# A graph-network kernel: the second node half's first layer, its rounding, lower part and aggregation in two halves of columns

## The chip, the cores and the metric

The kernel runs on one core of one Trainium2 chip. The metric is the device time of one execution in microseconds (us). The engines are called by the profile's names: PE is the matmul engine (PEld its weight loads), DVE the vector engine, ACT the scalar engine, POOL GpSimd, SP the engine that only issues transfers here. They run side by side, each through its own list of instructions in order, and wait for one another by semaphores.

## What is computed

Two layers of a graph network on 256 nodes with 512 features, over 4352 edges. The change sits wholly in the first layer. Cut to that layer:

```python
h = jnp.maximum(_layernorm(x, axis=-1), 0.0)
adj = zeros(256, 256); adj[src, dst] = 1; adj[dst, src] = 1
adj = adj + eye
dinv = 1.0 / sqrt(adj.sum(axis=1))
adj = adj * dinv[:, None] * dinv[None, :]
x = x + adj @ (h @ weight) + bias        # first layer (x @ weight is h @ weight here)
h = jnp.maximum(_layernorm(x, axis=-1), 0.0)
x = x + second_layer(h, src, dst, edge_attr_20, edge_weight, edge_attr_4, ...)
```

The second layer projects `h` to node channels, gathers them by edge, multiplies them by filters computed from the edge attributes, sums the products into the nodes (the scatter), and passes the sums through two more small layers.

## The kernel before, in words

The program is one block per engine, written out by hand: the order of instructions on each engine is the order of the code, and semaphores (the dictionary `q`, with `wait_ge` and `then_inc`) tie the engines together. There are no planners and no pools.

The 256 nodes are two halves of 128 partitions (NH = 2), numbered `a` or `b`; the 512 features are four blocks of 128 (KD = 4). PSUM is eight banks of 512 fp32 columns, and `pair0` to `pair3` are two banks each.

Before the change's place, DVE builds one-hot rows of the edges, PE multiplies them into the adjacency counts (`adjacency`, line 605), and PE transposes the normalised nodes into `h1T`. The first layer of node half 0 (`first_layer(0, ...)`, line 632, into `bank[0]`) is spread between the parts of the adjacency. Then, in this order:

- PE transposes the clipped counts (line 666). DVE makes of them the adjacency matrix `A` and the degrees (lines 465 and 469). PE meanwhile multiplies the first layer of node half 1, `first_layer(1, 0, KD)` (called at line 668): four matmuls of 512 columns in fp32 into `bank[1]`. A program matmul in fp32 shows as two MATMUL records, each with a weight load.
- POOL raises the degrees and variances to the power -0.5 (line 354): first `s1`, the scale of each row of `hW`, then `dinv`.
- ACT rounds `s1 * hW` of each half to fp32r, `hW_hi` (line 251), and DVE takes what the rounding left, `hW_lo` (line 479). Ahead of the latter DVE has two instructions of other work, `xb` (line 472) and `hYlo` (line 475).
- PE aggregates (line 674): for both parts and both halves `b` of the summed nodes, two matmuls of 512 columns (`a` = 0 and 1), into `bank[4]` and `bank[5]`. In the order of the code: high part of half 0, high part of half 1, low part of half 0, low part of half 1. Each of these four waits for its own piece. The last two matmuls raise `L0`.
- PE goes on with the product of two small weights (line 680) and the filters of the first two groups of edges (`filters(0)`, `filters(1)`, lines 649 and 652), and then waits for the next layer's input (`transposes`, line 688).
- DVE forms `x1`, the input of the second layer, once for each half (line 485), as `L0` rises. From there the second layer begins: `h2` (ACT line 257, DVE line 488), the sums of squares (lines 261 and 492), `h2T` (lines 263 and 496), the scale `s2` on POOL (lines 371 and 373), the node channels (line 695), their two parts `HL` (lines 277 and 504), and then the gather (line 721), the products and the scatter (line 733) over nine groups of edges.
- After the rounding ACT copies `y` out over the features for the products (`y_blocks(0, free)`, line 225), and POOL, after its powers, builds a quarter of a one-hot matrix (`node_onehots_late(3)`, line 358).

Of the kernel before, what the change touches and what calls it, by code (L numbers as in the profile page):

```python
# [5 lines left out]
def gnn_preln_kernel(nc, x, idx, dst_row, f_t, yr, w0, bias0, w1, w2, b2, w_in, w_o1s, w_o1vt, w_o2s, w_o2v,  # L6
                     out):
    fp32 = mybir.dt.float32
# [3 lines left out]
    ALU = mybir.AluOpType  # L12
    ACT = mybir.ActivationFunctionType

    P = 128
    N, D = x.shape
    NH = N // P
    KD = D // P
# [35 lines left out]
    with ctx:  # L54
        def sb(name, shape, dt=fp32):
            return ctx.enter_context(nc.sbuf_tensor(name, shape, dt))

        def sem(name):
            return ctx.enter_context(nc.semaphore(name))
# [7 lines left out]
        w0_sb = sb("w0_sb", [P, KD, D])  # L67
# [31 lines left out]
        h1T = sb("h1T", [P, NH, KD, P])  # L99
# [3 lines left out]
        A = sb("A", [P, NH, N], fp32r)  # L103
        deg = sb("deg", [P, 2 * NH])
        scales = sb("scales", [P, 2 * NH])
        dinv, s1 = scales[:, 0:NH], scales[:, NH:2 * NH]
        hW_hi = sb("hW_hi", [P, NH, D], fp32r)
        hW_lo = sb("hW_lo", [P, NH, D], fp32r)
# [29 lines left out]
        bank = [pair[i // 2][:, 512 * (i % 2):512 * (i % 2) + 512] for i in range(8)]  # L138
# [12 lines left out]
        q = {n: sem("s_" + n) for n in names.split()}  # L151
# [45 lines left out]
        def _(act):  # L197
# [48 lines left out]
            act.wait_ge(q["half"], 3)  # L246
            nc.scalar.activation(OdT[:, 1, E // 2:], gap, ACT.Relu, bias=one[:, 0:1], scale=-1.0).then_inc(q["OdTa"], 1)
            act.wait_ge(q["scales"], 1)
            for a in range(NH):
                act.wait_ge(q["hW"], a + 1)  # L250
                nc.scalar.activation(hW_hi[:, a, :], bank[a][:, :], ACT.Copy, scale=s1[:, a:a + 1]).then_inc(q["hW_hi"], 1)
            act.wait_ge(q["OdTa"], 1)
            act.wait_ge(q["adj"], 1)
            act.wait_ge(q["y"], 1)
# [3 lines left out]
                                 scale=-float(D)).then_inc(q["neg_h2"], 1)  # L258
# [16 lines left out]
            for a in range(NH):  # L275
                act.wait_ge(q["H"], a + 1)
                nc.scalar.activation(HL[:, a, 0, :], bank[4 + a][:, 0:C], ACT.Copy,
                                     scale=s2[:, a:a + 1]).then_inc(q["Hh"], 1)
# [126 lines left out]
        def _(dve):  # L405
# [68 lines left out]
            dve.wait_ge(q["hhi"], 2)  # L474
            nc.vector.tensor_tensor(hY[0:64, :], za[64:128, :], hY[64:128, :].bitcast(fp32), ALU.subtract).then_inc(q["hYlo"], 1)
            dve.wait_ge(q["scales"], 1)
            for a in range(NH):
                dve.wait_ge(q["hW_hi"], a + 1)
                nc.vector.scalar_tensor_tensor(hW_lo[:, a, :], bank[a][:, :], s1[:, a:a + 1],
                                               hW_hi[:, a, :].bitcast(fp32), ALU.mult, ALU.subtract).then_inc(q["hW_lo"], 1)  # L480
            dve.wait_ge(q["scales"], 2)
            dve.wait_ge(q["xb"], 1)
            for a in range(NH):
# [111 lines left out]
        def _(pe):  # L595
# [26 lines left out]
            for a in range(NH):  # L622
                pe.wait_ge(q["h1"], a + 1)
                for k in range(KD):
                    last = nc.tensor.transpose(bank[(6, 1)[a]][:, k * P:(k + 1) * P], h1[:, a, k * P:(k + 1) * P], id_sb)
# [3 lines left out]
            def first_layer(a, k0, k1):  # L629
                pe.wait_ge(q["h1T"], a + 1)  # L630
                for k in range(k0, k1):
                    last = nc.tensor.matmul(bank[a][:, :], h1T[:, a, k, :], w0_sb[:, k, :], start=(k == 0), stop=(k == KD - 1))  # L632
                if k1 == KD:
                    last.then_inc(q["hW"], 1)
# [29 lines left out]
            for a in range(NH):  # L664
                for b in range(NH):
                    last = nc.tensor.transpose(bT[:, a * N + b * P:a * N + (b + 1) * P], CI[:, b, a * P:(a + 1) * P], eye_sb[:, 0, 0:P])
            last.then_inc(q["CT"], 1)
            first_layer(1, 0, KD)

            for p, (part, ready) in enumerate(((hW_hi, "hW_hi"), (hW_lo, "hW_lo"))):  # L670
                for b in range(NH):
                    pe.wait_ge(q[ready], b + 1)
                    for a in range(NH):
                        last = nc.tensor.matmul(bank[4 + a][:, :], A[:, b, a * P:(a + 1) * P], part[:, b, :],  # L674
                                                start=(b == 0 and p == 0), stop=(b == NH - 1 and p == 1))
                        if b == NH - 1 and p == 1:
                            last.then_inc(q["L0"], 1)
            pe.wait_ge(d_o1v, 16)
            pe.wait_ge(d_o2v, 16)
# [106 lines left out]
            for a in range(NH):  # L786
# [4 lines left out]
                                 stop=True).then_inc(q["fin"], 1)  # L791
# [66 lines left out]
```

## Time and profile before

| | us |
|---|---|
| median of 3 runs | 71.69 (71.65 to 71.82) |
| the profiled execution | 71.83 |
| its span, first to last instruction | 69.8 |

In that execution PE is busy for 61.7 us (88% of the span), DVE for 60.1 (86%), ACT for 48.6 (70%) and POOL for 39.5 (57%). The granted clock of PE is full in the stretch of the change. The table of busy shares doesn't say what a change of a few matmuls is worth; this is read from the chain of work that ended last and from the order of time around the place.

### The profile page before, as it was taken

Reading aid. Unit: us, or ns where it says so; the run is one execution under the profiler, and the core shown is the slowest. Engines: PE = TensorE matmul, PEld = TensorE weight load, DVE = VectorE, ACT = ScalarE, POOL = GpSimd, SP = SyncE. Lnnn points to the kernel's source line nnn. Section 1 sums busy time; section 2 is a strip of 40 time slices with the busy share of each in tenths; the row PEclk is TensorE's granted clock in tenths of the full one; section 3 lists DMA queues with packets and bytes.
Section 4 is the critical chain, followed back from the end, with each engine's and each line's share of the span. In section 5 each row is a group of like instructions: output and inputs, shape, how many; then the busy total and the mean of one; then the engine's idle time right before and its main releaser. Section 6 shows DMA issues by size and latency. Waiting matters only on the chain.

```text
span 69.8 us, 1215 instructions
## 1 busy us (share of the span) xinstructions
PE 61.7 (88%) x407; PEld 48.6 (70%) x407; DVE 60.1 (86%) x124; ACT 48.6 (70%) x74; POOL 39.5 (57%) x46
## 2 busy tenths in 40 slices
PE   3999998999999999897998979999999999998340
PEld 1236754568834268796987969998898989997220
DVE  4599999999979968989999898989898999972760
ACT  0700059978999697967979999988696969732700
POOL 5000030000676989594799979999999988700000
PEclk9999999999999999999999999999999999999995
DMA  0899998984000000000000000000000000000044
GB/s 1 129 396 247 361 499 379 449 317 124 9 0 0 0 0 0 0 0 5 0 0 0 0 0 9 5 0 0 0 0 0 0 0 9 0 0 0 0 148 153
DMA packets 3049, 5.65 MB, mean 81 GB/s; under 512 B 540, under 2 KB 1936, under 8 KB 2916
## 3 DMA queue, kind: packets, MB, share of 16 engines
q1 hardware_dynamic: 2274, 5.14, 21.3%
q10 hardware_dynamic: 770, 0.44, 2.2%
q8 instruction: 3, 0.05, 0.3%
q14 instruction: 2, 0.02, 0.1%
HBM read 5.06 MB, written 0.52 MB: 80 GB/s over the span
## 4 chain that ended last, share of the span: by engine, by line
DVE 45%; PE 20%; issue 14%; ACT 13%; DMA 3%; DVEq 0%; ACTq 0%
ACT OsR L240 8%; DVE WQ L412 7%; DVE Os L412 7%; PE pair L632 5%; ACT w_sb L284 5%; DVE dst_bc L565 4%; PE pair L733 4%; PE pair L742 4%; DVE pair L514 3%; PE pair L674 3%; DMA idx_sb<-idx 3%; PE pair L721 3%; DVE w_sb L485 2%; DVE za L446 2%; DVE hX L449 2%
## 5 line engine op out<-in xcount | busy, mean ns | idle before, releaser
L733 PE MATMUL pair<-OsR,Mh 128*128 128x256 f32 x56 | 13.6, 281 | 0.0
L733 PE MATMUL pair<-OsR,Ml 128*128 128x256 f32 x56 | 13.6, 281 | 0.0
L721 PE MATMUL pair<-HL,OdT 128*128 128x256 f32 x68 | 10.1, 289 | 1.6 <-DVE dst_bc L565 0.7
L395 POOL TENSOR_TENSOR Ml<-dst_bc,Mh 128x512 fp32r<-128x512 f32 x8 | 10.4, 1305 | 1.1 <-ACT Mh L301 1.0
L721 PEld LDWEIGHTS pair<-HL,OdT 128*128 128x128 f32 x68 | 8.6, 188 | 2.8 <-issue 2.8
L733 PEld LDWEIGHTS pair<-OsR,Ml 128*128 128x128 f32 x56 | 10.5, 188 | 0.0
L733 PEld LDWEIGHTS pair<-OsR,Mh 128*128 128x128 f32 x56 | 10.5, 188 | 0.0
L605 PEld LDWEIGHTS pair<-WQ,Os 128*128 128x128 bf16 x68 | 6.8, 104 | 4.0 <-DVE WQ L412 1.8
L605 PE MATMUL pair<-WQ,Os 128*128 128x256 bf16 x68 | 9.4, 297 | 0.2 <-DVE WQ L412 0.2
L399 POOL TENSOR_TENSOR Ml<-dst_bc,Mh 128x512 fp32r<-128x512 f32 x7 | 9.2, 1309 | 0.0
L240 ACT ACTIVATE OsR<-Os 128x1024 fp32r<-128x1024 bf16 (+1 forms) x9 | 9.0, 999 | 0.0
L632 PE MATMUL pair<-w_sb,h1T 128*128 128x512 f32 x16 | 7.7, 601 | 0.3 <-ACT h1T L214 0.3
L305 ACT ACTIVATE Mh<-dst_bc 128x512 fp32r<-128x512 f32 (+1 forms) x9 | 5.5, 609 | 3.1 <-DVE dst_bc L565 3.0
L514 DVE TENSOR_TENSOR pair<-pair,w_sb 128x512 f32<-128x512 f32 (+1 forms) x10 | 6.2, 619 | 1.3 <-ACT w_sb L284 1.2
L358 POOL TENSOR_SCALAR OdT<-dst_bc,iota_c 128x1088 fp32r<-128x1088 int32 x2 | 6.1, 3054 | 1.6 <-DVE OdT L459 1.4
L341 POOL CAST b2p<-b_sb 96x128 bf16<-96x128 f32 x1 | 1.4, 1402 | 8.3 <-issue 8.3
L534 DVE TENSOR_TENSOR pair<-pair,WQ 128x512 f32<-128x512 f32 (+1 forms) x9 | 6.0, 662 | 0.1
L378 POOL TENSOR_TENSOR WQ<-WQ,y 128x256 f32<-128x256 f32 (+1 forms) x9 | 5.8, 652 | 0.1
L207 ACT ACTIVATE za<-pair 128x512 f32<-128x512 f32 (+1 forms) x3 | 1.4, 489 | 6.3 <-PE pair L613 6.3
L284 ACT ACTIVATE w_sb<-pair 128x512 f32<-128x512 f32 (+1 forms) x10 | 5.2, 518 | 0.8 <-PE pair L721 0.7
L412 DVE TENSOR_TENSOR Os<-iota_r,idp 128x512 bf16<-128x512 bf16 (+3 forms) x7 | 5.6, 796 | 0.0
L412 DVE TENSOR_TENSOR WQ<-iota_r,idp 128x512 bf16<-128x512 bf16 (+3 forms) x7 | 5.6, 796 | 0.0
(122 smaller groups left out, 140.2 us busy)
## 6 DMA issues: line engine op xcount, KB each, us to landing
dst_bc<-dst_row SPq DMA_DIRECT2D x1, 2176.0 KB, 12.9
w_sb<-w SPq DMA_DIRECT2D x1, 1024.0 KB, 8.1
x_sb<-x SPq DMA_DIRECT2D x1, 512.0 KB, 4.4
out<-x_sb SPq DMA_DIRECT2D x2, 192.0 KB, 1.9
f_sb<-f_t SPq DMA_DIRECT2D x1, 378.0 KB
b_sb<-bias SPq DMA_DIRECT2D x1, 256.0 KB, 13.1
w_sb<-w ACTq DMA_DIRECT2D x1, 128.0 KB, 4.1
out<-x_sb ACTq DMA_DIRECT2D x1, 128.0 KB, 1.9
```

What stands on the lines that cost most here:

```text
L240: nc.scalar.activation(OsR[:, g % RG, 0:n, :], Os[:, t0:t0 + n, :], ACT.Copy).then_inc(q["OsR"], 1)
L284: nc.scalar.activation(G_lo[:, g % RS, j0:j1, :, :], rows_of(g)[:, j0:j1, 1, :, :], ACT.Copy).then_inc(q["Glo"], 1)
L358: nc.gpsimd.tensor_scalar(OdT[:, 0, c * E // 4:(c + 1) * E // 4], dst_bc[:, c * E // 4:(c + 1) * E // 4], iota_c[:, 0:1], None, ALU.is_equ ...
L395: nc.gpsimd.tensor_tensor(Ml[:, o, 0:n, feats(1)], M[:, o, 0:n, feats(1)], Mh[:, o, 0:n, feats(1)].bitcast(fp32), ALU.subtract).then_inc(q ...
L399: nc.gpsimd.tensor_tensor(Ml[:, o, 0:n, feats(0)], M[:, o, 0:n, feats(0)], Mh[:, o, 0:n, feats(0)].bitcast(fp32), ALU.subtract).then_inc(q ...
L412: last = nc.vector.tensor_tensor(into[:, t0:t1, :].rearrange("p t (h k) -> p t h k", k=2), nodes, of_edge, ALU.is_equal)
L514: nc.vector.tensor_tensor(hi, hi, G_lo[:, g % RS, j0:j1, :, :].rearrange("p t c f -> p t (c f)"), ALU.add).then_inc(q["add"], 1)
L534: nc.vector.tensor_tensor(L, G, wq[:, :, 3:7, :], ALU.mult).then_inc(q["Q"], 1)
L605: last = nc.tensor.matmul(bank[4 + a][:, 0:N], Os[:, t, a * P:(a + 1) * P], Od[:, t, :], start=(t == 0), stop=(t == T - 1))
L632: last = nc.tensor.matmul(bank[a][:, :], h1T[:, a, k, :], w0_sb[:, k, :], start=(k == 0), stop=(k == KD - 1))
L721: last = nc.tensor.matmul(gpair[g % 2][:, j * 2 * C:(j + 1) * 2 * C], OdT[:, a, t * P:(t + 1) * P], HL[:, a, :, :], start=(a == 0), stop=( ...
L733: last = nc.tensor.matmul(bank[4 + b][:, 0:N], part[:, g % RG, j, feats(b)], OsR[:, g % RG, j, :], start=(TG * g + j == 0 and part is Mh), ...
```

## The change

The matmuls of node half 1 are cut into columns 0 to 255 and 256 to 511. The first layer of that half goes into the left halves of two banks, `bank[1]` and `bank[3]`, with eight matmuls of 256 columns where there were four of 512. ACT rounds the two pieces one after the other, and DVE takes their lower parts one after the other: three instructions each where there were two. PE aggregates the two parts of node half 0 as before with 512 columns, and those of node half 1 in four steps of two matmuls of 256 columns: high and low part of the left columns, then high and low part of the right ones. So the low part of node half 0 now stands ahead of the high part of node half 1. `hW`, `hW_hi` and `hW_lo` count to three.

```diff
+            act.wait_ge(q["hW"], 1)
+            nc.scalar.activation(hW_hi[:, 0, :], bank[0][:, :], ACT.Copy, scale=s1[:, 0:1]).then_inc(q["hW_hi"], 1)
+            for half in range(2):
+                act.wait_ge(q["hW"], 2 + half)
+                nc.scalar.activation(hW_hi[:, 1, half * D // 2:(half + 1) * D // 2], bank[(1, 3)[half]][:, 0:D // 2], ACT.Copy,
+                                     scale=s1[:, 1:2]).then_inc(q["hW_hi"], 1)
...
+            dve.wait_ge(q["hW_hi"], 1)
+            nc.vector.scalar_tensor_tensor(hW_lo[:, 0, :], bank[0][:, :], s1[:, 0:1],
+                                           hW_hi[:, 0, :].bitcast(fp32), ALU.mult, ALU.subtract).then_inc(q["hW_lo"], 1)
+            for half in range(2):
+                cols = slice(half * D // 2, (half + 1) * D // 2)
+                dve.wait_ge(q["hW_hi"], 2 + half)
+                nc.vector.scalar_tensor_tensor(hW_lo[:, 1, cols], bank[(1, 3)[half]][:, 0:D // 2], s1[:, 1:2],
+                                               hW_hi[:, 1, cols].bitcast(fp32), ALU.mult, ALU.subtract).then_inc(q["hW_lo"], 1)
...
-            first_layer(1, 0, KD)
+            pe.wait_ge(q["h1T"], NH)
+            for half in range(2):
+                cols = slice(half * D // 2, (half + 1) * D // 2)
+                for k in range(KD):
+                    last = nc.tensor.matmul(bank[(1, 3)[half]][:, 0:D // 2], h1T[:, 1, k, :], w0_sb[:, k, cols], start=(k == 0),
+                                            stop=(k == KD - 1))
+                last.then_inc(q["hW"], 1)
 
             for p, (part, ready) in enumerate(((hW_hi, "hW_hi"), (hW_lo, "hW_lo"))):
-                for b in range(NH):
-                    pe.wait_ge(q[ready], b + 1)
+                pe.wait_ge(q[ready], 1)
+                for a in range(NH):
+                    nc.tensor.matmul(bank[4 + a][:, :], A[:, 0, a * P:(a + 1) * P], part[:, 0, :], start=(p == 0), stop=False)
+            for half in range(2):
+                cols = slice(half * D // 2, (half + 1) * D // 2)
+                for p, (part, ready) in enumerate(((hW_hi, "hW_hi"), (hW_lo, "hW_lo"))):
+                    pe.wait_ge(q[ready], 2 + half)
                     for a in range(NH):
-                        last = nc.tensor.matmul(bank[4 + a][:, :], A[:, b, a * P:(a + 1) * P], part[:, b, :],
-                                                start=(b == 0 and p == 0), stop=(b == NH - 1 and p == 1))
-                        if b == NH - 1 and p == 1:
+                        last = nc.tensor.matmul(bank[4 + a][:, cols], A[:, 1, a * P:(a + 1) * P], part[:, 1, cols],
+                                                start=False, stop=(half == 1 and p == 1))
+                        if half == 1 and p == 1:
                             last.then_inc(q["L0"], 1)
```

PE before, from the transposes of the counts (line 666) to the product of small weights (line 680). `pair0` holds `bank[0]` and `bank[1]`, `pair1` holds `bank[2]` and `bank[3]`, `pair2` holds `bank[4]` and `bank[5]`; a row is one program matmul, or several with an x.

```order
L666 MATMUL pair1<-eye_sb,warmup 128x128 x3
L632 MATMUL pair0<-w0_sb,h1T 128x512 [waits s_h1T]
L632 MATMUL pair0<-w0_sb,h1T 128x512 x3
L674 MATMUL pair2<-hW_hi,A 128x512 [waits s_hW_hi]
L674 MATMUL pair2<-hW_hi,A 128x512
L674 MATMUL pair2<-hW_hi,A 128x512 [waits s_hW_hi]
L674 MATMUL pair2<-hW_hi,A 128x512
L674 MATMUL pair2<-hW_lo,A 128x512 [waits s_hW_lo]
L674 MATMUL pair2<-hW_lo,A 128x512
L674 MATMUL pair2<-hW_lo,A 128x512 [waits s_hW_lo]
L674 MATMUL pair2<-hW_lo,A 128x512
L680 MATMUL pair0<-o2v_sb,o1vt_sb 128x128 [waits dma_o2v,dma_o1v]
```

The same place of PE after the change.

```order
L679 MATMUL pair0<-w0_sb,h1T 128x256 x3
L679 MATMUL pair1<-w0_sb,h1T 128x256 x4
L686 MATMUL pair2<-hW_hi,A 128x512 [waits s_hW_hi]
L686 MATMUL pair2<-hW_hi,A 128x512
L686 MATMUL pair2<-hW_lo,A 128x512 [waits s_hW_lo]
L686 MATMUL pair2<-hW_lo,A 128x512
L692 MATMUL pair2<-hW_hi,A 128x256 [waits s_hW_hi]
L692 MATMUL pair2<-hW_hi,A 128x256
L692 MATMUL pair2<-hW_lo,A 128x256 [waits s_hW_lo]
L692 MATMUL pair2<-hW_lo,A 128x256
L692 MATMUL pair2<-hW_hi,A 128x256 [waits s_hW_hi]
L692 MATMUL pair2<-hW_hi,A 128x256
```

The third matmul of the aggregation waited for a second piece of `hW_hi`; now it waits for the first piece of `hW_lo`. Behind it stand eight matmuls of 256 columns (six are shown) where there were four of 512.

DVE after the change, from its last work ahead of the lower parts to `x1`; before, there were two instructions of 512 columns in the place of the three that write `hW_lo`.

```order
L478 TENSOR_TENSOR hY<-za,hY 64x1152 [waits s_hhi]
L481 SCALAR_TENSOR_TENSOR hW_lo<-pair0,scales,hW_hi 128x512 [waits s_hW_hi,s_scales]
L486 SCALAR_TENSOR_TENSOR hW_lo<-pair0,scales,hW_hi 128x256 [waits s_hW_hi]
L486 SCALAR_TENSOR_TENSOR hW_lo<-pair1,scales,hW_hi 128x256 [waits s_hW_hi]
L492 SCALAR_TENSOR_TENSOR w0_sb,xsum<-pair2,scales,f_sb 128x512 [waits s_L0,s_xb,s_scales]
```

The first piece of `hW_lo` keeps its width and its place behind `hY`; only the second one is cut.

## Rows read from the trace of the kernel before

**Rows 1.** The chain that ended last, in order of time: start us, us, what
```profile
20.46 3.49 PE pair L632 x8
...
23.96 0.73 PE pair L674 x2
...
24.73 1.45 PE pair L674 x5
...
26.31 1.44 DVE w_sb L485 x4
```
**Rows 2.** Order of time, ACT, DVE and POOL around the rounding: start us, us, engine
```profile
21.61 2.94 POOL L354 TENSOR_TENSOR scales<-deg,neghalf 128x2 f32<-128x2 f32 x2 [0.89 <-POOL b2p L347]
22.64 1.35 DVE L475 TENSOR_TENSOR hY<-za,hY 64x1152 fp32r<-64x1152 f32 x1
23.22 1.46 ACT L251 ACTIVATE hW_hi<-pair,scales 128x512 fp32r<-128x512 f32 x2 [0.60 <-POOL scales L354]
23.99 0.69 ACT L251 ACTIVATE hW_hi<-pair,scales 128x512 fp32r<-128x512 f32 x1
24.03 0.75 DVE L479 SCALAR_TENSOR_TENSOR hW_lo<-pair,scales,hW_hi 128x512 fp32r<-128x512 f32 x1
24.71 0.75 DVE L479 SCALAR_TENSOR_TENSOR hW_lo<-pair,scales,hW_hi 128x512 fp32r<-128x512 f32 x1
24.58 2.20 ACT L225 ACTIVATE WQ<-y 128x2400 f32<-128x2400 f32 x1
```
**Rows 3.** Order of time, single matmuls of the aggregation on PE, and the last two together
```profile
24.73 0.51 PE L674 MATMUL pair<-hW_hi,A 128*128 128x512 f32 x1
25.55 0.40 PE L674 MATMUL pair<-hW_lo,A 128*128 128x512 f32 x1
25.78 0.63 PE L674 MATMUL pair<-hW_lo,A 128*128 128x512 f32 x2
```
**Rows 4.** Order of time, matmuls of 256 columns back to back, in the scatter
```profile
58.08 0.28 PE L733 MATMUL pair<-OsR,Mh 128*128 128x256 f32 x1
58.20 0.28 PE L733 MATMUL pair<-OsR,Ml 128*128 128x256 f32 x1
...
60.45 1.11 PE L742 MATMUL pair<-OsR,Mh 128*128 128x256 f32 x8
```
**Rows 5.** One line's instructions: duration ns min/median/max, first and last start us, forms
```profile
L688 PE MATMUL pair<-id_sb,h x8: 272/278/329, 27.9 to 28.7; 128*128 128x128 f32 x8
...
L782 PE MATMUL pair<-b_sb,o1s_sb x2: 376/428/480, 63.7 to 64.1; 64*128 64x256 f32 x2
```
**Rows 6.** Groups by form, ACT and DVE copies from PSUM: busy, mean ns | idle before
```profile
L284 ACT ACTIVATE w_sb<-pair 128x512 f32<-128x512 f32 x7 | 4.1, 580 | 0.3 <-PE pair L721 0.3
L284 ACT ACTIVATE w_sb<-pair 128x256 f32<-128x256 f32 x3 | 1.1, 375 | 0.5 <-PE pair L721 0.4
L514 DVE TENSOR_TENSOR pair<-pair,w_sb 128x512 f32<-128x512 f32 x7 | 4.9, 699 | 1.2 <-ACT w_sb L284 1.2
L514 DVE TENSOR_TENSOR pair<-pair,w_sb 128x256 f32<-128x256 f32 x3 | 1.3, 433 | 0.1
```
**Rows 7.** Order of time, what follows the first layer
```profile
27.10 0.72 ACT L257 ACTIVATE h<-w_sb,xsum 128x512 f32<-128x512 f32 x1 [0.33 <-DVE w_sb L485]
27.75 0.28 PE L652 MATMUL pair<-w_lo,hY 128*128 128x256 f32 x1
29.18 0.19 POOL L371 TENSOR_SCALAR ve<-sq 128x2 f32<-128x2 f32 x1 [0.77 <-DVE f_sb L492]
31.44 0.35 DVE L504 SCALAR_TENSOR_TENSOR HL<-pair,s,HL 128x128 fp32r<-128x128 f32 x1 [0.26 <-issue]
31.71 0.35 DVE L504 SCALAR_TENSOR_TENSOR HL<-pair,s,HL 128x128 fp32r<-128x128 f32 x1
32.29 0.19 PEld L721 LDWEIGHTS pair<-HL,OdT 128*128 128x128 f32 x1 [0.53 <-issue]
```
**Rows 8.** Busy us of each engine in one stretch: PE, PEld, DVE, ACT, POOL, then PEclk
```profile
23.96:26.31 2.35, 2.31 (x9) 1.60 (x10) 1.48 (x4) 2.32 (x2) 2.16 (x2) 1.00 0.00 0
```

More of the change, by code:

```diff
@@ L248, in _ @@
             act.wait_ge(q["scales"], 1)
-            for a in range(NH):
-                act.wait_ge(q["hW"], a + 1)
-                nc.scalar.activation(hW_hi[:, a, :], bank[a][:, :], ACT.Copy, scale=s1[:, a:a + 1]).then_inc(q["hW_hi"], 1)
+            act.wait_ge(q["hW"], 1)
[4 more added lines that the diff above has]
+                                     scale=s1[:, 1:2]).then_inc(q["hW_hi"], 1)
             act.wait_ge(q["OdTa"], 1)
@@ L476, in _ @@
             dve.wait_ge(q["scales"], 1)
[L477 to L480, printed above, removed]
+            dve.wait_ge(q["hW_hi"], 1)
[6 more added lines that the diff above has]
+                                               hW_hi[:, 1, cols].bitcast(fp32), ALU.mult, ALU.subtract).then_inc(q["hW_lo"], 1)
             dve.wait_ge(q["scales"], 2)
```

## The prediction

> **What bounds the kernel now.** I read first the chain that ended last, then the order of time on each engine around its stretch, and last the rows by form for what a half-wide instruction costs. The page says that PE and DVE are both busy for nearly nine tenths of the span; that decides nothing here, because in this stretch each waits for the other in turn.
>
> In the chain [rows 1] the reader is to see that the place is on it from end to end: the first layer of node half 1 (from 20.46), the first two matmuls of the aggregation (23.96), a short wait, the rest of the aggregation (24.73), then `x1` on DVE (26.31). PE's clock is full there (1.00) [rows 8]. The next question is what ended the wait ahead of 24.73. ACT's first rounding starts at 23.22, when POOL's first power is done [rows 2], so it ends at 23.22 + 0.69 = 23.91 and PE starts its first two aggregation matmuls at 23.96. ACT's second rounding starts at 23.99, as soon as the first layer's last matmul has come out at 23.95, ends at 24.68, and PE goes on at 24.73 [rows 1, 2]. On DVE `hY` ends at 22.64 + 1.35 = 23.99; the first lower part runs 24.03 to 24.78 and the second 24.71 to 25.46 [rows 2]. PE reaches the second lower part's first matmul at 25.78 [rows 3], 0.3 after it was ready, so before the change DVE isn't waited for in this stretch.
>
> **The change part by part.** *The first layer.* A matmul record of 512 fp32 columns takes 3.49 / 8 = 0.436 at most [rows 1]. A record of 256 fp32 columns stands in line 782: 0.376 where it follows another [rows 5]. What a record shows over its spacing is the way through the array: matmuls of the scatter follow each other by 58.20 - 58.08 = 0.12 and last 0.28, so 0.16 [rows 4]; at 512 columns it is 0.40 less 25.78 - 25.55 = 0.23, about the same [rows 3]. So fp32 at half width costs 0.376 - 0.16 = 0.21, and sixteen of them 3.4, as much as the eight before. Its weight loads are hidden in that, as the spacing of 0.12 in the scatter shows loads to go through faster. The left columns are ready by about 22.2, the right ones at 23.95 to 24.0. If each record cost 0.03 more, the layer would end 0.5 later, at 24.45; its successors on PE take 0.12 + 2 x 0.23 and would end at 25.0, against the 24.83 at which, below, PE must wait anyway. That is the cover, about 0.3, and without it only some 0.1 would be lost. Cost taken: 0.
>
> *The rounding on ACT.* Half a width saves 0.580 - 0.375 = 0.205 on a copy from PSUM [rows 6], so a piece of 256 costs 0.69 - 0.20 = 0.48. An instruction of ACT starts 0.10 ahead of its forerunner's end where it has nothing to wait for (24.68 against 24.58) [rows 2]. So: 23.22 to 23.91, 23.81 to 24.29, 24.19 to 24.67. The old wait of 0.18 for the first layer (23.99 instead of 23.81) goes, and pays for the third instruction. What is ready last is ready when it was, at 24.68. `y_blocks` behind it starts when it did, and it has slack: ACT idles 0.33 before 27.10 [rows 7]. Cost: 0.
>
> *The lower parts on DVE.* The first keeps its width and its start, since `hY` and the first rounding stand ahead of it: 24.03 to 24.78. Half a width saves 0.699 - 0.433 = 0.266 [rows 6], so a piece costs 0.75 - 0.27 = 0.48; instructions overlap by 0.07 (24.78 against 24.71) [rows 2]. The pieces end at 25.20 and 25.61, 0.15 later than the one did, and DVE then only waits for PE.
>
> *The aggregation on PE, which is on the path.* After its first two matmuls PE has ended its issue by 24.54, as before. Its next instruction now wants the first `hW_lo`, not the second `hW_hi`. That piece is done at 24.78 instead of 24.68, and with the same lag of 0.05 PE restarts at 24.83, **0.10 later** than at 24.73. What then stands ahead of the end of the first half of `L0`:
>
> - before, five matmuls of 512 columns: 5 x 0.233 = 1.165 (the records at 24.73, ..., 25.55, 25.78 [rows 3]; 0.233 is a fourth of the way from the second, at 24.73 + 0.51 - 0.40 + 0.233 = 25.08, to the last, at 25.78 + 0.63 - 0.40 = 26.01);
> - after, two of 512 and seven of 256 columns: 2 x 0.233 + 7 x 0.118 = 1.292. The 0.118 is the scatter's spacing with a weight load for each matmul, (1.11 - 0.28) / 7 [rows 4], exact to some 0.003.
>
> So the cut costs **0.13** here: a matmul of half the width takes 0.118 and not 0.1165, which is nothing, but the last piece for `bank[4]` now stands behind two narrow matmuls for `bank[5]` more than before. In columns, 5 x 512 = 2560 become 2 x 512 + 7 x 256 = 2816, one narrow matmul more. Check from the other end: restart 24.83, load ahead of the first matmul 0.11 (0.51 against 0.40), 1.29, and 0.16 through the array gives 26.40; the same sum for before gives 24.73 + 0.11 + 1.165 + 0.16 = 26.17, and `x1` starts at 26.31. The pieces of DVE are ready in time: PE wants the left lower part near 25.6 (ready 25.20) and the right one near 26.0 (ready 25.61), so those waits cost 0, with 0.3 to 0.4 to spare.
>
> The sum is 0.10 + 0.13 = **0.23 later for `x1`**, and nothing gained on the path: the wait that the change removes (second rounding) is replaced by one that ends later.
>
> *What follows.* `x1` starts at 26.54 instead of 26.31. PE, having issued its last matmul 0.11 later, would be free for the transposes at 27.98 instead of 27.87 (27.75 + 0.12), but they need ACT's `h2`, done at 27.10 + 0.72 = 27.82 and now at 28.05, so they follow by 0.2. POOL waits for DVE's sum of squares (0.77 idle before 29.18) [rows 7], so `s2`, `HL` and the gather follow as well. I find no later wait that ends on something which doesn't come from `x1`. The whole rest moves by 0.23.
>
> *Bounds.* From below: a restart after 0.04 and spacings of 0.115 give 0.20. From above: in `HL` the second lower part ends at 31.71 + 0.35 = 32.06, and PE's load comes at 32.29, a lag of 0.23 instead of 0.05 [rows 7]. Nothing shows why; PE waited for no DVE lower part in this stretch before, so it could hold here too, and adds 0.18: 0.41. I take 0.05, since it is what the same instruction saw from ACT (23.91 to 23.96, 24.68 to 24.73), in the same stretch.
>
> **The rivals.**
>
> *A. The delay is taken up later (not slower).* Ahead of `HL` DVE idles 0.26 with no releaser in the profile (before 31.44), and PE's loads 0.53 before 32.29 [rows 7]. If one of them ends on something fixed in time, a delay of 0.23 vanishes in it, and from 0.26 on it would not. Against it: ACT's rounding of `HL`, POOL's `s2` and the products of POOL around it all come from `x1`. Result: 71.69 + 0 to 0.1, 71.7 to 71.8, near the noise.
>
> *B. A gain.* It would take PE to find the first `hW_lo` ready when its second matmul is issued (24.54), so DVE 0.3 earlier. Then the aggregation would run without a wait from 23.96: PE goes on at 24.54 instead of 24.73, with the load of 0.11 hidden, which less the 0.13 leaves a gain of 0.06 to 0.17, about 71.6. Against it `hY` ends at 23.99 and the first rounding at 23.91. A shift of the later groups into a happier order, of one short wait of 0.26, would give 71.69 + 0.23 - 0.26 = 71.66 and at best two of them 71.4.
>
> *C. Narrow matmuls cost their weight load.* If the seven narrow ones took the 0.19 that a load lasts [rows 7] instead of 0.118, `x1` would be 7 x 0.07 = 0.5 later still: 71.69 + 0.23 + 0.50 = 72.42. The scatter's 0.12 with just such pairs speaks against it [rows 4]. The Trainium skill, TensorE: Matmul & The Clock Gate, section on the back-to-back issue gap, says of streams of load and matmul that they take about 81 ns each at 128 columns and 131 ns at 512, so that width would hardly matter; a straight line between these gives an estimate of 98 ns at 256, and the aggregation would lose 2 x 131 + 7 x 98 - 5 x 131 = 293 ns where my sum has 127, for a time of 72.08. The rows speak against its figure at 512 columns here, 233 ns.
>
> **How the numbers follow.** The likeliest is the rigid shift: 71.69 + 0.23 = **71.92**, with its bounds 71.85 to 72.10 (its own range with the noise 71.8 to 72.15). Against the profiled execution it is 71.83 + 0.23 = 72.06; that one lies 0.14 above the median, at the top of the three runs (71.65 to 71.82). I give the shift 0.66, rival A 0.16, rival B 0.12, rival C 0.06. A difference of 0.3%, 0.215, is about what a measurement can tell from none. The shift, at 0.23, lies just above it, so I split it: 0.46 over and 0.20 within. That gives slower 0.46 + 0.06 = 0.52, within 0.20 + 0.16 + 0.02 of B = 0.38, faster 0.10. The range is 71.5 to 72.2: it leaves out C and the ends of B and of the shift.
>
> **What would show it.** Right: the first `hW_lo` ends within 0.05 of 24.8; PE's record behind the first two matmuls of the aggregation starts 0.05 after it; the narrow records follow by 0.12; ACT's last rounding ends near 24.7; `x1` starts near 26.5; and from there to the last group of the scatter each row stands 0.2 later. Wrong: an `x1` near 26.3, a wait of PE for the second or third `hW_lo`, a first layer that ends much after 24.0, or an `x1` at 26.5 with a gather that starts when it did, which would be rival A.

## The result and the profile after

The changed kernel takes 72.06 us in the median (71.86 to 73.27, 6 runs) beside 71.74 for the one before (71.65 to 71.82). The ratio is 1.0045, with a 95% interval of 1.0023 to 1.0067: 0.32 us slower (0.16 to 0.48). A second set of runs gave 1.0033 (1.0020 to 1.0046), 0.24 us. The forecast was 0.23.

In the first profile of the changed kernel (73.27 us) and in e10's below the granted clock of PE is at half for 3.4 us from about 32.5; such executions take over 1 us longer, occur in the kernel before too, and are left out of the ratios. So the rows below are from a second profile of the same kernel (e8 below), with a span of 69.9 us. Its line numbers are three to eighteen higher than those of before. Its rows on DVE from 14.41 up to `hY` lie 0.07 earlier than before, ahead of anything that the change touches (the profiles don't settle why); so times of different kernels are compared by their distance from the start of `hY` on DVE (22.64 before, 22.57 here).

The chain that ended last, in order of time (start us, us, what), to be read beside [rows 1]:

```profile
23.90 0.06 issue
23.96 0.76 DVE hW_lo L481
24.72 0.04 issue
24.76 0.74 PE pair L686 x2
25.50 0.95 PE pair L692 x8
26.46 0.01 issue
26.46 0.77 DVE w_sb L492 x2
```

The first `hW_lo` on DVE has entered the chain, where PE's first layer and first two aggregation matmuls stood before. PE restarts at 24.76, 0.04 after it. The same stretch in order of time (start us, us, engine, line), beside [rows 2, 3]:

```profile
22.57 1.35 DVE L478 TENSOR_TENSOR hY<-za,hY 64x1152 fp32r<-64x1152 f32 x1
23.15 0.69 ACT L250 ACTIVATE hW_hi<-pair,scales 128x512 fp32r<-128x512 f32 x1 [0.59 <-POOL scales L357]
23.74 0.83 ACT L253 ACTIVATE hW_hi<-pair,scales 128x256 fp32r<-128x256 f32 x2
23.96 0.75 DVE L481 SCALAR_TENSOR_TENSOR hW_lo<-pair,scales,hW_hi 128x512 fp32r<-128x512 f32 x1
24.45 2.21 ACT L225 ACTIVATE WQ<-y 128x2400 f32<-128x2400 f32 x1
24.63 0.87 DVE L486 SCALAR_TENSOR_TENSOR hW_lo<-pair,scales,hW_hi 128x256 fp32r<-128x256 f32 x2
24.76 0.30 PEld L686 LDWEIGHTS pair<-hW_lo,A 128*128 128x128 f32 x2 [0.57 <-DVE hW_lo L481]
25.34 0.40 PE L692 MATMUL pair<-hW_hi,A 128*128 128x256 f32 x2
26.05 0.40 PE L692 MATMUL pair<-hW_lo,A 128*128 128x256 f32 x2
26.46 0.75 DVE L492 SCALAR_TENSOR_TENSOR w_sb<-pair,scales,f_sb 128x512 f32<-128x512 f32 x1 [0.97 <-PE pair L692]
28.03 1.12 PE L706 MATMUL pair<-id_sb,h 128*128 128x128 f32 x8
32.47 0.59 PE L739 MATMUL pair<-HL,OdT 128*128 128x256 f32 x3 [0.36 <-DVE HL L511]
```

The reader is to see four things. ACT's two half-wide roundings take 0.83 together and end at 24.57, and DVE's two lower parts end at 25.50: both are done before PE takes them (the last one's matmuls start at 26.05), and no row of PE names either in its wait. PE's weight loads waited 0.57 for the first `hW_lo`, where the wait for the second `hW_hi` was 0.47 before (last row below). Eight narrow matmuls take 0.95, 0.119 each. And `x1` starts 3.89 behind the start of `hY`, where before it was 26.31 - 22.64 = 3.67: **0.22 later**. The transposes (28.03) stand 5.46 behind it where they stood 5.24, and the gather (32.47) 9.90 where it stood 9.68 (its load at 32.29 in [rows 7], its matmul 0.03 later). The delay arrives there whole. The wait before the change:

```profile
24.73 0.30 PEld L674 LDWEIGHTS pair<-hW_hi,A 128*128 128x128 f32 x2 [0.47 <-ACT hW_hi L251]
```

The two halves of the first layer, one line of the program, as single instructions (ns min/median/max):

```profile
L679 PEld LDWEIGHTS pair<-w_sb,h1T x16: 190/190/192, 20.2 to 23.3; 128*128 128x128 f32 x16
L679 PE MATMUL pair<-w_sb,h1T x16: 379/379/435, 20.2 to 23.5; 128*128 128x256 f32 x16
```

The sixteen records of 379 ns start 0.215 apart; the last one ends at 23.90, where before it was 23.95: the cut layer ends 1.33 behind `hY` and the whole one ended 1.31 behind it.

### The profile page after: what moved, and what is told of

It reads as the page before. It is cut to its first block, busy times and chain, and to the rows that moved or that the text cites. A ratio compares the mean times of both kernels' runs of the same rounds, so it can differ in the third digit from the quotient of the medians.

```text
span 71.2 us, 1241 instructions
## 1 busy us (share of the span) xinstructions
PE 62.7 (88%) x419; PEld 51.4 (72%) x419; DVE 60.2 (84%) x125; ACT 48.6 (68%) x75; POOL 39.9 (56%) x46
## 4 chain that ended last, share of the span: by engine, by line
DVE 38%; PE 31%; ACT 15%; issue 9%; DMA 3%; DVEq 0%; ACTq 0%
PE pair L751 9%; PE pair L739 9%; DVE WQ L415 7%; DVE Os L415 7%; ACT OsR L240 5%; PE pair L760 4%; ACT w_sb L287 3%; PE pair L713 3%; DMA idx_sb<-idx 3%; DVE dst_bc L572 2%; DVE za L449 2%; DVE hX L452 2%; PE pair L659 2%; DVE hY L478 2%; DVE st L434 2%
## 5 line engine op out<-in xcount | busy, mean ns | idle before, releaser
L739 PE MATMUL pair<-HL,OdT 128*128 128x256 f32 x68 | 11.0, 306 | 1.2 <-DVE HL L511 0.4
L739 PEld LDWEIGHTS pair<-HL,OdT 128*128 128x128 f32 x68 | 9.6, 208 | 2.3 <-issue 2.3
L612 PE MATMUL pair<-WQ,Os 128*128 128x256 bf16 x68 | 8.8, 282 | 0.8 <-DVE WQ L415 0.8
L308 ACT ACTIVATE Mh<-dst_bc 128x512 fp32r<-128x512 f32 (+1 forms) x9 | 5.5, 609 | 3.0 <-DVE dst_bc L572 3.0
L338 POOL TENSOR_TENSOR y<-yr_sb 128x136 f32<-128x136 f32 x1 | 1.2, 1242 | 8.0 <-DMA yr_sb<-yr 8.0
L304 ACT ACTIVATE Mh<-dst_bc 128x512 fp32r<-128x512 f32 (+1 forms) x9 | 5.4, 603 | 0.0
```

The source lines that it names most:

```text
L612: last = nc.tensor.matmul(bank[4 + a][:, 0:N], Os[:, t, a * P:(a + 1) * P], Od[:, t, :], start=(t == 0), stop=(t == T - 1))
L739: last = nc.tensor.matmul(gpair[g % 2][:, j * 2 * C:(j + 1) * 2 * C], OdT[:, a, t * P:(t + 1) * P], HL[:, a, :, :], start=(a == 0), stop=( ...
```

## The experiments

Each was timed against the kernel before on the same chip. A ratio is turned into us at 71.7. The last three columns are from one profiled execution each; the end is that of the last instruction, and e10's is left out. In the short diffs `piece` and `step` are helpers that wait for one piece and issue its one matmul or its two (`a` = 0 for bank 4, `a` = 1 for bank 5); `L` and `R` are the left and right columns of node half 1.

| | edit | ratio (95% interval) | `x1` after `hY` | gather after `hY` | end after `hY` |
|---|---|---|---|---|---|
| before | | | 3.67 | 9.68 | 47.11 |
| e8 | changed, second set | 1.0033 (1.0020 to 1.0046) | 3.89 | 9.90 | 47.33 |
| e1 | changed, high parts first | 0.9984 (0.9964 to 1.0003) | 3.52 | 9.53 | 46.99 |
| e2 | before, low 0 ahead of high 1 | 1.0036 (1.0021 to 1.0050) | 3.76 | 9.87 | 47.29 |
| e3 | changed, aggregation as before | 1.0005 (0.9992 to 1.0019) | 3.63 | 9.63 | 47.06 |
| e4 | before, four matmuls more | 1.0073 (1.0060 to 1.0086) | 4.11 | 10.14 | 47.55 |
| e5 | changed, bank 4 first | 1.0027 (1.0011 to 1.0043) | 3.53 | 9.71 | 47.12 |
| e6 | before, bank 4 first | 1.0002 (0.9992 to 1.0011) | 3.51 | 9.69 | 47.12 |
| e7 | e2, `o1s` on POOL moved | 1.0038 (1.0020 to 1.0055) | 3.74 | 9.75 | 47.18 |
| e9 | e6, product moved | 0.9983 (0.9971 to 0.9996) | 3.52 | 9.53 | 46.94 |
| e10 | e5, product moved | 0.9982 (0.9971 to 0.9993) | 3.54 | 9.55 | - |
| e11 | e1, product moved | 0.9974 (0.9963 to 0.9985) | 3.51 | 9.52 | 46.93 |

The changed kernel's second set ran with e5 to e7:

> The changed kernel once more, for a profile at full clock and more runs beside the others. Theory: x1 0.23 later than before, the end 0.2 to 0.35 later.

**Is it the order or the cut?** Three kernels undo one part each. The first keeps the cut and puts the high parts first again:

```diff
-high 0, low 0, high L, low L, high R, low R
+high 0, high L, high R, low 0, low L, low R
```

> The changed kernel with one edit: PE takes the pieces of the aggregation in the old order, all high parts first (half 0 wide, then left and right columns of half 1), then the low parts (half 0 wide, left, right). Theory (the cost of the change is the order, which puts a wait for the first low part where a wait for the second high part was, plus one narrow matmul more ahead of the end): the left high part is ready at 24.29, so PE doesn't stop at 24.54; two wide and four narrow matmuls are issued by 25.01, after the first low part (24.78); the right low part, ready at 25.61 to 25.66, is wanted at about 25.7. x1 starts near 26.15 instead of 26.31: 0.1 to 0.2 faster than before, so 71.55 to 71.65 and 0.4 less than the changed kernel. Rival (the cost comes from the narrow matmuls and the third instructions themselves, whatever the order): as slow as the changed kernel, +0.2 to +0.4.

Measured: 0.9984 (0.9964 to 1.0003), 0.11 less, with an interval that still touches no change; clearly under the changed kernel's 1.0033. In its order of time (`hY` starts at 22.40):

```profile
23.72 1.24 PE L686 MATMUL pair<-hW_hi,A 128*128 128x512 f32 x6
24.80 1.11 PE L686 MATMUL pair<-hW_lo,A 128*128 128x512 f32 x6
25.92 0.75 DVE L492 SCALAR_TENSOR_TENSOR w_sb<-pair,scales,f_sb 128x512 f32<-128x512 f32 x1 [0.59 <-PE pair L686]
```

The twelve matmuls run without a wait between them, and `x1` starts 3.52 behind `hY`, 0.15 earlier than before and 0.37 earlier than in the changed kernel. The cost isn't in the narrow instructions; there are as many of them here.

The second kernel changes the order alone, with nothing cut:

```diff
-high 0, high 1, low 0, low 1
+high 0, low 0, high 1, low 1
```

> The kernel before with one edit: nothing is cut, but PE takes high and low part of half 0 first, then high and low part of half 1, all 512 columns wide. Theory: PE restarts on the first low part, 0.10 later than before, and five wide matmuls stand ahead of the end as before: x1 0.10 later, total +0.10 (71.84), of the changed kernel's 0.23 the smaller part. Rival (order costs nothing, the narrow matmuls are all of it): +0.0. Rival (the whole excess over before, 0.3, is the order): +0.3.

`x1` came 0.09 later, as expected, but the total rose by 0.26 (0.15 to 0.36), more than the 0.10. The profile has the rest one instruction later, in the order of time:

```profile
27.80 0.59 DVE L488 TENSOR_SCALAR h<-w_sb,xsum 128x512 f32<-128x512 f32 x1
27.81 0.29 POOL L367 TENSOR_SCALAR o1s_sb<-o1s_sb 32x128 f32<-32x128 f32 x1
```

In the kernel before, the same two stand at 27.78 (DVE, 0.49) and 27.88 (POOL, 0.53):

```profile
27.78 0.49 DVE L488 TENSOR_SCALAR h<-w_sb,xsum 128x512 f32<-128x512 f32 x1
27.88 0.53 POOL L367 TENSOR_SCALAR o1s_sb<-o1s_sb 32x128 f32<-32x128 f32 x1
```

Where DVE started well ahead, POOL's instruction was the long one; where they started together, DVE's `h2` was, and `h2` is on the path: the gather comes 0.19 later though `x1` came only 0.09 later. In the changed kernel POOL's starts first and `h2` behind it, and neither is longer:

```profile
27.80 0.29 POOL L370 TENSOR_SCALAR o1s_sb<-o1s_sb 32x128 f32<-32x128 f32 x1
27.93 0.49 DVE L495 TENSOR_SCALAR h<-w_sb,xsum 128x512 f32<-128x512 f32 x1
```

To test this, POOL's small instruction was moved to its end, where nothing stands beside it:

```diff
-            nc.gpsimd.tensor_scalar(o1s_sb[F:2 * F, :], ...)      # behind node_onehots_late(3)
+            nc.gpsimd.tensor_scalar(o1s_sb[F:2 * F, :], ...)      # behind the loop over groups
```

> The order-only kernel (e2) with one edit: the small scaling of o1s on POOL is moved from behind its one-hots (27.81 in e2) to its end. In e2 it started 0.01 behind h2 on DVE (27.80), and that h2 took 0.59 instead of 0.49. Theory (the two shared an access in SBUF, and the 0.10 of it is what e2 lost over its 0.10 for the order): h2 takes 0.49 again, and the total is 0.1 less than e2, +0.1 over before. Rival (h2's length has another cause or isn't on the path): total as e2, +0.26.

`h2` took 0.49 again and the gather moved from 9.87 to 9.75, as the theory has it. In the profiles the end moves with it, from 47.29 behind `hY` to 47.18. The total didn't confirm it: 1.0038 (1.0020 to 1.0055) beside 1.0036. Of the eight times behind this ratio six lie at 71.82 to 71.87 and two at 72.2 and 72.3; the profile caught one of the latter, with a chain that starts at a transfer of `f_t` (done at 8.39), and `hY` at 23.03 instead of 22.57, far ahead of the edit. So that the clash lengthens `h2` rests on e2's profile (in all the others `h2` takes 0.49); that it makes the kernel slower is not shown by the totals.

The third keeps the cut first layer, roundings and lower parts, and takes the aggregation of before:

```diff
-low 0 (512), high L, low L, high R, low R (256 each)
+high 1 (512), low 0 (512), low 1 (512)
```

> The changed kernel with the aggregation of before: first layer, rounding and low parts of half 1 are still cut in two, but PE takes four wide steps in the old order (high 0, high 1, low 0, low 1), and waits for the last piece of each. Theory: cutting the producers costs nothing and gains nothing: the right high part ends at 24.67 as the whole one did, the right low part at 25.61, wanted at 25.78. Total +0.0 (within 0.1). Rival (the cut first layer or rounding costs): the excess of the changed kernel, +0.2 to +0.4, stays.

Measured 1.0005 (0.9992 to 1.0019): no change, and `x1` within 0.04. Cutting the producers costs nothing. It gains nothing either.

**Does a delay here reach the end?** Four matmuls without use were put ahead of the last two of the aggregation in the kernel before (their results are read by nobody):

```diff
+            for _ in range(4):
+                nc.tensor.matmul(bank[0][:, 0:D // 2], A[:, 0, 0:P], hW_hi[:, 0, 0:D // 2], start=True, stop=True)
```

> The kernel before with four extra matmuls of 256 columns (into a bank that nobody needs then) right ahead of the last two of the aggregation. Measures how a delay at this place reaches the end. Theory (rigid shift): 4 x 0.118 = 0.47 later x1 and 0.47 later end, 72.2. Rival A (taken up by the idle stretch of 0.26 ahead of HL or the 0.53 ahead of the gather): x1 0.47 later, but the end only 0.2 later or less.

```profile
25.68 0.63 PE L682 MATMUL pair<-hW_hi,A 128*128 128x256 f32 x4
26.15 0.63 PE L673 MATMUL pair<-hW_lo,A 128*128 128x512 f32 x2
26.68 0.75 DVE L485 SCALAR_TENSOR_TENSOR w_sb<-pair,scales,f_sb 128x512 f32<-128x512 f32 x1 [1.29 <-PE pair L673]
```

They take 26.15 - 25.68 = 0.47; `x1` comes 0.44 later, the gather 0.46, the end 0.52 (0.43 to 0.62). The delay reaches the end whole, and rival A, a stretch that takes it up, falls: the idle time ahead of `HL`, 0.28 here, moves along.

In the changed kernel that idle time did something else, which the prediction hadn't foreseen:

```profile
31.25 0.34 DVE L511 SCALAR_TENSOR_TENSOR HL<-pair,s,HL 128x128 fp32r<-128x128 f32 x1
31.46 0.37 ACT L280 ACTIVATE HL<-pair,s 128x128 fp32r<-128x128 f32 x1 [0.39 <-PE pair L713]
31.87 0.35 DVE L511 SCALAR_TENSOR_TENSOR HL<-pair,s,HL 128x128 fp32r<-128x128 f32 x1 [0.27 <-ACT HL L280]
```

The first `HL` starts 8.68 behind `hY`, where before it was 31.44 - 22.64 = 8.80 with 0.26 of idle time ahead of it [rows 7]. The idle time is gone, here and in the five other kernels with three lower parts on DVE (e1, e3, e5, e10, e11); the profiles don't say why. Yet nothing is won by it. The second `HL`, which the gather waits for too, waits for ACT's second rounding of `HL` (done at 31.46 + 0.37 = 31.83), and that waits for PE's node channels, so for `x1`.

**Is it what stands ahead of bank 4's end?** In the changed kernel the eight narrow matmuls were sorted by bank, and in the kernel before the four low ones:

```diff
-a = 0, 1 in each of high L, low L, high R, low R
+a = 0 in high L, low L, high R, low R, then a = 1 in the same
```

> The changed kernel with one edit: in the four narrow steps of half 1, all four matmuls for bank 4 come first, then the four for bank 5. The total of PE's work, the cut and the restart on the first low part stay; only the number of narrow matmuls ahead of the end of bank 4 falls from seven to four. Theory (x1 waits for what stands ahead of the end of bank 4): bank 4 is done 3 x 0.118 = 0.35 earlier, x1 at 26.2 on the scale of the kernel before (26.31), so 0.35 less than the changed kernel and 0.1 less than the one before, about 71.6. Rival (the cost lies in the number of narrow matmuls, or x1 of bank 5 decides): as slow as the changed kernel.

> The kernel before, nothing cut, with one edit: of the four matmuls with low parts the two for bank 4 come first, then the two for bank 5. One wide matmul less stands ahead of the end of bank 4, but the second low part is then wanted at 25.43 and is ready at 25.46, with the lag 25.51. Theory: x1 0.15 to 0.2 earlier than before (26.1 to 26.15), total 71.55. If e5 and this one come out alike, the cut into columns brings nothing that the order of the banks doesn't bring alone. Rival (the halved pieces are needed to gain): 71.7.

`x1` did what was expected of it, 0.36 earlier than in the changed kernel in e5 and 0.16 earlier than before in e6. The totals did not: 1.0027 (1.0011 to 1.0043) and 1.0002 (0.9992 to 1.0011). My expectation had followed `x1` alone. PE's rows in e6, in order of time, show what is late next (the chain below counts a piece of PE to the end of its last record, so it has the transposes at 28.02):

```profile
23.88 1.51 PE L672 MATMUL pair<-hW_hi,A 128*128 128x512 f32 x4
26.24 0.39 PE L686 MATMUL pair<-o2v_sb,o1vt_sb 128*128 128x128 f32 x2
27.76 0.97 PEld L694 LDWEIGHTS pair<-id_sb,h 128*128 128x128 f32 x8
27.86 1.07 PE L694 MATMUL pair<-id_sb,h 128*128 128x128 f32 x8
```

The weight loads of the transposes start at 27.76, 5.20 behind `hY`, but the matmuls only at 27.86, 5.30 behind it (5.24 before). e6's chain names what held them:

```profile
26.40 0.22 PE pair L686 x2
26.63 0.22 PE pair L649
26.84 0.47 PE pair L652 x4
27.32 0.23 PE pair L649
27.55 0.47 PE pair L652 x4
28.02 0.93 PE pair L694 x8
```

Sorting by bank doesn't give PE less to do: the product and the two filter groups are issued until 27.86, and the transposes of the second layer stand behind them in its queue. `h2` was there at 26.87 + 0.72 = 27.59 and waited. So the product (0.22) was moved behind the transposes, into a wait of PE:

```diff
-            nc.tensor.matmul(bank[1][:, 0:B], o1vt_sb[:], o2v_sb[:], ...)      # behind the aggregation
             transposes(0)
             transposes(1)
+            nc.tensor.matmul(bank[1][:, 0:B], o1vt_sb[:], o2v_sb[:], ...)
```

> e6 (before, bank 4 first) with one edit: the product of the two small weights on PE moves from ahead of the filters to behind the transposes of the second layer, where PE waits 0.33 for ACT. In e6 x1 came 0.16 earlier and the transposes came no earlier, since PE was at its filters until 27.87. Theory (e6's gain was held up by PE's own queue): PE is free 0.22 earlier, the transposes follow h2 and the gather comes 0.16 earlier than before: 0.15 less, 71.5 to 71.55. Rival (something else held it): as e6, no gain.

> e5 (the changed kernel, bank 4 first) with the same edit. In e5 x1 came 0.35 earlier than in the changed kernel, but PE ended the filters at 28.0. Theory: PE is free 0.22 earlier and the gather comes 0.15 earlier than in the kernel before; total 0.1 to 0.2 less than before, 71.5 to 71.6. Rival: as e5, +0.1 to +0.2.

> e1 (cut in columns, all high parts first) with the same edit. In e1 PE idled 0.17 for h2 ahead of the transposes, so its queue didn't hold it. Theory: the edit brings nothing here, the total stays 0.1 to 0.2 under before (71.5 to 71.6). Rival (PE's queue held e1 as well): 0.1 more gain, 71.4.

e9 gives 0.9983 (0.9971 to 0.9996) and e10 0.9982 (0.9971 to 0.9993): both gain 0.12 or so on the kernel before. In e9 the transposes start as soon as `h2` is there (26.88 + 0.72 = 27.60), and the product fits behind them:

```profile
26.09 0.75 DVE L485 SCALAR_TENSOR_TENSOR w_sb<-pair,scales,f_sb 128x512 f32<-128x512 f32 x1 [0.70 <-PE pair L672]
26.88 0.72 ACT L257 ACTIVATE h<-w_sb,xsum 128x512 f32<-128x512 f32 x1 [0.18 <-DVE w_sb L485]
27.66 1.12 PE L691 MATMUL pair<-id_sb,h 128*128 128x128 f32 x8
28.62 0.39 PE L705 MATMUL pair<-o2v_sb,o1vt_sb 128*128 128x128 f32 x2
32.10 1.07 PE L727 MATMUL pair<-HL,OdT 128*128 128x256 f32 x7 [0.36 <-DVE HL L504]
```

e11, the cut kernel with all high parts first and the product moved, has the lowest ratio: 0.9974 (0.9963 to 0.9985), 0.19 us under the kernel before; its interval overlaps those of e9 and e10. Its `x1` and gather stand where e1's did (3.51 and 9.52 against 3.52 and 9.53), so the edit brought nothing there, as expected; so e1 and e11 are two measurements of about the same thing, and their intervals overlap. All three kernels that are clearly faster have the gather at 9.52 to 9.55. One of them, e9, cuts nothing.

## Why the prediction was right

- *Only the aggregation is on the path, the cut producers cost nothing:* right. e3 has all of them cut, at 1.0005. Single sizes: a rounding of 256 columns takes 0.474 (0.48 said), a lower part 0.477 (0.48), the first layer's records are 0.215 apart (0.21).
- *PE restarts 0.10 later, on the first low part:* right. It is 24.76 - 22.57 = 2.19 behind `hY`, and 24.73 - 22.64 = 2.09 before; the releaser is the one named, and the lag is 0.04 to 0.05. The upper bound with a lag of 0.23, from `HL`, didn't occur. e2, with this step alone, has `x1` 0.09 later.
- *0.13 for what stands ahead of bank 4's end:* right. `x1` in the changed kernel is 3.89 and in e2 3.76, a difference of 0.13, and taking three narrow matmuls away from there (e5) brings `x1` 0.36 earlier, 3 x 0.12.
- *Narrow matmuls at 0.118:* right, 0.119, beside 0.233 for wide ones. Rival C is out. The Trainium skill, TensorE: Matmul & The Clock Gate, section on the back-to-back issue gap, has about 81 ns at 128 columns and 131 ns at 512 for streams of load and matmul; the trace doesn't agree for these fp32r operands, since half the width takes half the time.
- *A rigid shift of the rest:* right for this kernel: 0.22 at `x1`, 0.22 at the transposes, 0.22 at the gather, 0.24 to 0.32 at the end. e4 shows it for a delay of twice the size. One row went another way: the first `HL` on DVE came 0.12 earlier, where each row was to stand 0.2 later, and only the second one's wait for ACT kept the gather at 0.22. But it isn't a law for both signs: an earlier `x1` gains nothing (e6) unless PE's own queue is done earlier too, as it is in e1 and e9. The prediction had seen that the transposes had two releasers within 0.05 of each other (27.87 and 27.82) and used it only for the delay.
- *Rival B:* it said that a gain needs the low part on DVE 0.3 earlier. This was too narrow. Within the new cut PE has four narrow matmuls with high parts that are ready, 0.47 of work, to put ahead of the low part; e1 does that, and `x1` comes 0.15 earlier.
- *Not settled:* why the totals of e2, e5 and e7 are higher than their profiles. In the profiled executions the end keeps the gather's distance: e2's gather is 0.19 late and its end 0.18, e7's 0.07 and 0.07, e5's 0.03 and 0.01. The totals are +0.26 (0.15 to 0.36), +0.27 (0.14 to 0.39) and +0.19 (0.08 to 0.31). So what is missing doesn't lie behind `hY` in these traces. The start of `hY`, which no edit touches, lies between 22.40 (e1) and 23.03 (e7) in the profiled executions, a spread larger than what is missing; with one profile for each kernel this is a candidate and not shown.

## What to carry to other kernels

Where a step is cut in pieces so that a consumer can start sooner, the gain is in the order in which the consumer takes them: put every piece that is ready ahead of the first that isn't, and count what stands ahead of the end that the next engine waits for. Here the same pieces were 0.2 to 0.3 us slower in one order and 0.1 to 0.2 faster in the other (the 0.2 with the product moved as well, which changed neither `x1` nor the gather). Before an earlier result is expected to help, look at the queue of the engine that takes it next: with two releasers within 0.05 a delay passes whole and a gain doesn't.

## What the runs showed of the hardware

A small instruction on POOL (32x128, 0.29 by itself) and one on DVE (128x512, 0.49 by itself) can lengthen one another when they overlap, and which of them grows hangs on their starts. Where DVE's had started 0.10 to 0.26 ahead, in eight profiles (before, e1, e3, e5, e6, e9, e10, e11), DVE's kept its 0.49 and POOL's took 0.38 to 0.53: it ended 0.15 behind the end of DVE's each time, however far it had come. Where DVE's had started only 0.01 ahead (e2), DVE's took 0.59 and POOL's 0.29. With POOL's 0.13 ahead (the changed kernel), both kept their length though they overlapped by 0.16. With POOL's moved away (e7), DVE's was at 0.49. The runs don't say by what mechanism.
